# Building the one-hot tables of a mixture-of-experts placement column by column on VectorE and GpSimd

## The reference, cut to what matters

```
logits = xf @ Wg
idx = jnp.argmax(logits, axis=-1)
final = jnp.zeros_like(xf)
for e in range(N_EXPERTS):
    y = geglu(xf, W1[e], W2[e], W3[e])
    final = final + jnp.where((idx == e)[:, None], y, 0.0)
return (shared + final).reshape(B, T, C)
```

## Time and profile before

| | |
|---|---|
| median of 3 runs | 1822.69 us (1822.34 to 1825.03) |
| the profiled execution's own time | 1825.35 us |
| span of that execution in the profile | 1823.4 us |
| TensorE busy | 1508.2 us, 83% of the span |
| VectorE busy | 1206.4 us, 66% |
| GpSimd busy | 1014.5 us, 56% |
| ScalarE busy | 953.0 us, 52% |
| placing in the first shared stage | 72 to 103 us of the span |
| placing in the second shared stage | 1020 to 1052 us |
| placing in the routing of the top-2 mixture | 1240.4 to 1262.8 us |

### The profile page before, as it was taken

How to read it: one execution, slowest core, us unless ns; L and a number is a source line. 1 busy time by engine, 2 the same in 40 slices (tenths; PEclk the granted TensorE clock), 3 DMA queues, 4 the chain that set the end, 5 groups by cost and what they waited for, 6 DMA issues and landing times. The chain is left out here.

```text
span 1823.4 us, 36275 instructions
## 1 busy us (share of the span) xinstructions
PE 1508.2 (83%) x9925; PEld 1265.2 (69%) x9988; DVE 1206.4 (66%) x2802; ACT 953.0 (52%) x1970; POOL 1014.5 (56%) x1326
## 2 busy tenths in 40 slices
PE   6889956699999999999978899943999378809993
PEld 4559953478888888888765579942999256708993
DVE  5535556689999999999745545557566368724566
ACT  2213334678787777878733223342666267616662
POOL 2135742188888888888862146644543474553442
PEclk9999976799999999999988999955999689959997
DMA  7001130101010110101106011160222121112224
GB/s 248 1 24 32 47 107 29 37 26 38 26 38 26 30 33 26 37 26 38 37 1 202 1 29 41 41 201 7 69 66 57 39 53 32 36 36 62 64 62 157
DMA packets 112428, 98.53 MB, mean 54 GB/s; under 512 B 25312, under 2 KB 88960, under 8 KB 112288
## 3 DMA queue, kind: packets, MB, share of 16 engines
q1 hardware_dynamic: 97424, 68.84, 12.7%
q0 software_dynamic: 13632, 27.98, 5.5%
q10 hardware_dynamic: 1232, 0.04, 0.0%
HBM read 50.24 MB, written 44.47 MB: 52 GB/s over the span
## 5 line engine op out<-in xcount | busy, mean ns | idle before, releaser
L886 PE MATMUL ps<-gT,w_slot 128*128 128x128 f32 x1760 | 242.4, 282 | 4.5 <-ACT gT L920 3.2
L898 PE MATMUL ps<-w,inner_slot 128*128 x1760 | 235.5, 277 | 5.5 <-DVE inner_slot L976 3.2
L886 PEld LDWEIGHTS ps<-gT,w_slot 128*128 128x128 f32 x1760 | 219.4, 196 | 13.7 <-issue 6.0
L898 PEld LDWEIGHTS ps<-w,inner_slot 128*128 128x128 f32 x1760 | 213.9, 192 | 10.5 <-issue 9.8
L1966 DVE SCALAR_TENSOR_TENSOR xbc<-ps,cw,xbc 128x1021 f32<-128x1021 f32 x132 | 168.3, 1275 | 16.8 <-ACT xbc L1845 14.7
L966 DVE TENSOR_TENSOR hb<-ps,b 128x512 f32<-128x512 f32 x142 | 98.2, 691 | 105.3 <-PE ps L886 96.6
L831 POOL DMA_INDIRECT rows_in<-xn_rows,slot_token x117 | 113.6, 971 | 81.0 <-PE ps L874 56.5
L1720 PE MATMUL ps<-xnT,win 128*128 128x512 f32 x256 | 134.2, 650 | 27.1 <-DVE xbc L1966 21.5
L2158 POOL TENSOR_TENSOR xd<-t,xd 128x256 f32<-128x256 f32 x128 | 94.3, 736 | 86.6 <-DVE t L2001 86.6
L1771 PEld LDWEIGHTS ps<-XB,LM 128*128 128x128 f32 x1024 | 136.1, 194 | 6.8
L838 POOL DMA_INDIRECT y_rows<-y,slot_row x78 | 91.1, 1168 | 81.0 <-DVE y L983 79.8
(11 more groups left out here) (336 smaller groups left out, 4011.0 us busy)
## 6 DMA issues: line engine op xcount, KB each, us to landing
sorted_rows<-blank SPq DMA_DIRECT2D x33, 516.0 KB, 4.8
w<-in_L_ffn_W SPq DMA_DIRECT2D x5, 2048.0 KB, 10.7
xn_rows<-xn SPq DMA_DIRECT2D x24, 256.0 KB, 4.3
xn<-y_rows SPq DMA_DIRECT2D x24, 256.0 KB, 5.2
rows_in<-sorted_rows SPq DMA_DIRECT2D x71, 64.5 KB, 1.8
y_rows<-y SPq DMA_DIRECT2D x71, 64.0 KB, 1.5
rows_in<-xn_rows,slot_token POOLq DMA_INDIRECT x149, 2.6
x<-in_L_attn_x SPq DMA_DIRECT2D x8, 256.0 KB, 6.4
```

Of the source, the lines that this page charges most:

```text
L886: ins = nc.tensor.matmul(h1[:, u, b * P:(b + 1) * P], w[:, b * P:(b + 1) * P], k.gT[:, r, :], start=True, stop=True)
L898: ins = nc.tensor.matmul(py[:, q % 2, :], k.inner_slot[:, q % RING, b * P:(b + 1) * P], w_dn[:, ds(e * (FB * D) + b * D, D)], start=(b == ...
```

## The change

`match` and ScalarE's part are gone. VectorE makes each column on its own: one operation on the list of slot numbers compares with `hi` and multiplies by the partition number straight into `oh_slot`, a second compares lanes. GpSimd does the same with the tile number as a constant. So GpSimd no longer waits for VectorE batch by batch: it waits once until `hi` is there, which VectorE signals behind `route_positions`, and then only for `placed`. A batch is now 8 VectorE operations in place of 2, 4 on GpSimd in place of 1, and none on ScalarE.

```diff
@@ route: vector
             route_positions(k, do, top)
+            dve.sem_inc(k.matched.sem, 1)
             for n in range(NB):
-                match_vector(k, dve, n, slots)
+                match_vector(k, dve, n, slots, top)
@@ route: scalar
             nc.scalar.activation(k.small[:, 0:NT], k.small[:, 0:NT], ACT.Exp).then_inc(expd.sem, 1)
-            for n in range(NB):
-                match_lanes(k, act, n, slots, top)
@@
-def match_vector(k, dve, n, slots):
+def match_vector(k, dve, n, slots, top):
     V, r = k.nc.vector, n % 2
-    cols = slice(n * GRP, (n + 1) * GRP)
-    dve.wait_ge(k.lanes_put.sem, k.lanes_put.at(n - 1))
-    dve.wait_ge(k.tiles_put.sem, k.tiles_put.at(n - 1))
-    V.tensor_tensor(k.match[:, r, :, 0:slots], bcast(k.iota_bf[:, 0:slots], 1, GRP), bcast(k.hi[:, cols], 2, slots),
-                    ALU.is_equal).then_inc(k.matched.sem, 1)
     dve.wait_ge(k.placed.sem, k.placed.at(n - 1))
-    V.tensor_tensor(k.oh_lane[:, r, :, :], bcast(k.iota_bf[:, 0:P], 1, GRP), bcast(k.lo[:, cols], 2, P),
-                    ALU.is_equal).then_inc(k.onehot.sem, 1)
-def match_lanes(k, act, n, slots, top):
-    r = n % 2
-    act.wait_ge(k.matched.sem, k.matched.at(n + 1))
-    act.wait_ge(k.placed.sem, k.placed.at(n - 1))
-    k.nc.scalar.activation(k.oh_slot[:, r, :, 0:slots], k.match[:, r, :, 0:slots], ACT.Copy,
-                           scale=k.lane[:, top - 1:top]).then_inc(k.lanes_put.sem, 1)
+    for j in range(GRP):
+        c = n * GRP + j
+        V.tensor_scalar(k.oh_slot[:, r, j, 0:slots], k.iota_bf[:, 0:slots], k.hi[:, c:c + 1], k.lane[:, top - 1:top],
+                        ALU.is_equal, ALU.mult)
+        ins = V.tensor_scalar(k.oh_lane[:, r, j, :], k.iota_bf[:, 0:P], k.lo[:, c:c + 1], None, ALU.is_equal)
+    ins.then_inc(k.onehot.sem, 1)
 
 def match_tiles(k, pool, n, slots):
     r = n % 2
-    pool.wait_ge(k.matched.sem, k.matched.at(n + 1))
+    if n == 0:
+        pool.wait_ge(k.matched.sem, k.matched.at(1))
     pool.wait_ge(k.placed.sem, k.placed.at(n - 1))
-    k.nc.gpsimd.tensor_tensor(k.oh_slot[:, r, :, slots:2 * slots], k.match[:, r, :, 0:slots],
-                              bcast(k.tile_of[:, n * GRP:(n + 1) * GRP], 2, slots), ALU.mult
-                              ).then_inc(k.tiles_put.sem, 1)
+    for j in range(GRP):
+        c = n * GRP + j
+        ins = k.nc.gpsimd.tensor_scalar(k.oh_slot[:, r, j, slots:2 * slots], k.iota_bf[:, 0:slots], k.hi[:, c:c + 1],
+                                        float(c + 1), ALU.is_equal, ALU.mult)
+    ins.then_inc(k.tiles_put.sem, 1)
@@ place_tensor
     pe.wait_ge(k.onehot.sem, k.onehot.at(n + 1))
-    pe.wait_ge(k.lanes_put.sem, k.lanes_put.at(n + 1))
     pe.wait_ge(k.tiles_put.sem, k.tiles_put.at(n + 1))
@@ shared: vector
                 if u == 15:
                     route_positions(k, do, 1)
+                    dve.sem_inc(k.matched.sem, 1)
                 if 16 <= u < 24:
-                    match_vector(k, dve, u - 16, slots)
+                    match_vector(k, dve, u - 16, slots, 1)
@@ shared: scalar
-                if 17 <= u < 25:
-                    match_lanes(k, act, u - 17, slots, 1)
```

More of the change, by code:

```diff
@@ L459, in place_counters @@
     k.onehot, k.placed, k.place_own = (k.counter(f"place_{n}") for n in ("onehot_ready", "done", "step"))
-    k.matched, k.lanes_put, k.tiles_put = (k.counter(f"place_{n}") for n in ("matched", "lanes_put", "tiles_put"))
+    k.matched, k.tiles_put = (k.counter(f"place_{n}") for n in ("matched", "tiles_put"))
 def close_places(k, batches, top):
-    for s in (k.onehot, k.placed, k.matched, k.lanes_put, k.tiles_put):
+    for s in (k.onehot, k.placed, k.tiles_put):
         s.close(batches)
+    k.matched.close(1)
@@ L2263, in setup @@
     k.oh_lane, k.oh_slot = S("oh_lane", [P, 2, GRP, P], BF16), S("oh_slot", [P, 2, GRP, 2 * SLOTS2], BF16)
-    k.iota_bf, k.match = S("iota_bf", [P, P], BF16), S("match", [P, 2, GRP, SLOTS2], BF16)
+    k.iota_bf = S("iota_bf", [P, P], BF16)
     k.wg0, k.wg1, k.bg = S("wg0", [P, NE]), S("wg1", [P, NE]), S("bg", [P, NE])
```

## The result

The changed kernel took 1834.36 us (median of 10 runs, 1829.17 to 1837.96). The kernel before, run beside it, took 1824.92. The ratio is **1.0042, 95% interval [1.0028, 1.0057]**: slower by 0.4%, which is some 7.7 us. The forecast was 4.3 us faster.

What follows compares the result with a forecast made beforehand. ScalarE's weighing was taken to stall TensorE in the shared stages, VectorE to bound the routing. Shared stages -8.2, routing +3.9, together -4.3: 1822.69 to 1818.4 us; range 1810 to 1833, the forecast's own 1812 to 1824.

Steps and rivals of the forecast that it cites:

- The step that failed: Routing: GpSimd's four operations per batch take at most 1.36 us, under M, if the extra [128, 1] operand is cheap.
- M: VectorE's time from first to last operation of a batch: forecast 1.70 us in the routing, 1.55 in the shared stage.
- rival D: Routing: GpSimd becomes the bound; 0.5 an operation gives 1823.2 us, 0.7 gives 1836; chance 20%.
- the 1.01 for a power of four elements: Profile row of a GpSimd power, 1.01 us, beside which VectorE's four operations took 1.08, no more than their own sum.
- The lower bound for free [128, 1] operands: VectorE's batch if its [128, 1] operands cost nothing: given as 4 x 0.24 = 0.96 us.
- rival C: New VectorE operations cost 1.0 ns per element, batch 2.02 + 0.25 and 1.89 + 0.15: 1831.5 us; chance 10%.
- The contention of 0.25 and 0.15: What GpSimd's four operations add to VectorE's batch: 0.25 us in the routing, 0.15 in the shared stage.
- Rival B: GpSimd holds up every new VectorE operation for its whole duration, batch 2.80 and 2.57: 1844 us; chance 9%.
- Forecast -4.1: Each shared stage: TensorE waits for VectorE's table instead of ScalarE's weighing, gain 10.3 - 4M = 4.1 us.
- the 1.0 that the forecast called lost behind the last placing: Shared stage: `inner(25)` stands behind the table of experts, so 1.0 us of the last placing's 1.29 is lost.
- rival E: Shared stages give nothing because something unseen ends them, and the routing's +3.9 remains: 1826.6 us; chance 6%.
- The forecast's 0.4: End of the routing: L369 no longer meets GpSimd's last table, saving 0.4 us.

Runs made afterwards that it cites:

- kernel 1: Changed kernel plus a stretch ahead of all work timing series of eight single operations on GpSimd, VectorE, then both; whole took 1866.56 us, left out of comparisons.
- kernel 6: Changed kernel plus a stretch of GpSimd alone, series of eight varying output offset, column and constants; series take 4.12 to 4.75 us, no whole time given.
- kernel 4: Changed kernel, but in the routing VectorE makes the tile part of two of four columns instead of GpSimd; stretch 41.7 to 34.5, execution 1823.9 us (one run).
- kernel 5: Changed kernel, but GpSimd's routing operation multiplies instead of comparing, so its tables are wrong; routing stretch 41.7 to 28.6 us, one run 1816.0.
- kernel 8: New tables in shared stages, old in routing, where ScalarE also weighs two of four tile columns; 1810.77 us, ratio 0.9921 against the kernel before the change.
- kernel 2: Changed kernel with the old tables put back in the routing, new ones kept in both shared stages; 1813.57 us, ratio 0.9939 against the kernel before the change.

## Why the prediction was wrong, point by point

**The step that failed** is the one on GpSimd in the routing: "GpSimd: alone, one input of 4 elements takes 0.23; 71 elements at 0.0016 add 0.11: four are at most 1.36, under M, if the extra [128, 1] operand is cheap." It took the price per element from a product of two inputs and gave it to a comparison, and called the sum a maximum. The operand that it named as its condition is indeed cheap. The forecast was 0.34 an operation; the comparing form alone takes 0.52 (kernel 1), and the routing's 64 took 0.604 each. Of the 0.26 that was missing, about half is the price of an element (71 times 0.0034 in place of 0.0016), 0.05 the fixed part (0.28 for 0.23), and 0.09 comes on top in place, part of which the series with changing constants show too (kernel 6). Four take 2.25 to 2.53, over M, so GpSimd sets the pace. The prediction had named this as a sign of being wrong: a GpSimd operation over 0.4.

This is rival D, which had 20%. Its working from that point was right in kind: at 38.65 / 64 = 0.604 an operation, its formula gives 16 x (2.42 - 1.43) - 0.4 = +15.4 for the routing, and +14.3 was measured. The missing 1.1 is more than explained by `route_experts`, which D left behind the tables and which is hidden beside GpSimd's last ones (-2.1). That this one term is the cause is shown from both sides: kernel 4 took half of it away and kernel 5 made it cheap, and the routing fell to 34.5 and 28.6.

I had a row that ought to have widened the bound, the 1.01 for a power of four elements, and used it for VectorE's contention and for the rival's chance, not for this term.

**VectorE's batch, M.** The uncontended part was right to 0.04: 1.44 and 1.41 forecast, 1.48 measured with 71 slots and 1.44 with 39 (95.98 to 97.51, less 0.09 for the overlap, where GpSimd rests). Single operations were forecast at 0.29 and 0.25 and take 0.30 and 0.25 in the probe. (The lower bound for free [128, 1] operands is 4 x 0.21 = 0.84 by the prediction's own terms, not 0.96; nothing else uses it.) The Trainium skill (VectorE: DVE Perf Modes, "The perf-mode tier table") gives a bf16 `tensor_scalar` four elements a cycle. These durations fit it, with the prediction's fixed parts, to 0.02; rival C and its 1.0 ns per element are out. The contention of 0.25 and 0.15 was too much: with GpSimd at work all the time the batch was 1.48 in kernel 5, as alone. In the change itself it was mostly 1.67 in the first half of the routing (1244.25 to 1246.01, less 0.09) and 1.53 to 1.56 in most of the second. So the comparison on GpSimd disturbs VectorE there and the product of kernel 5 does not. It lies in GpSimd's shadow and costs nothing.

**Rival B, the lock.** The Trainium skill (SBUF — State Buffer, "Who interferes with whom") says that a VectorE operation in a two-port mode and GpSimd exclude each other for the whole instruction. For the new forms no run shows that: 12 pairs beside GpSimd's eight take 0.39 each against 0.37 alone. Whole-instruction exclusion would have added 8 x 0.54 to them. In kernel 5 GpSimd's operation goes from 0.32 to 0.37 and VectorE's batch stays as it is alone. The same section says that a VectorE instruction with two SBUF inputs contends with GpSimd's reads; with that the old form agrees, in the earlier trace rows and in kernel 8.

**Shared stage.** Forecast -4.1, measured -3.7, and the parts can be checked against start times. From the first placing to the eighth: 29.18 before (73.40 to 102.58), 24.19 now (76.85 to 101.04), -5.0. From the end of the positions to the first: 3.49 before, 3.75 now, +0.3, where the forecast had no change. From the eighth to `slot_row`: 4.34 before, 5.34 now, +1.0, which is the 1.0 that the forecast called lost behind the last placing. There `inner(25)` stands behind `route_experts`, and TensorE waits for it:

```profile
104.59 0.24 DVE L380 CAST slot_expert<-erow 128x156 int32<-128x156 f32 x1
104.86 0.69 DVE L600 TENSOR_TENSOR inner<-gl,ps 128x512 f32<-128x512 f32 x1
...
105.61 1.12 PE L705 MATMUL ps<-xnT,w 128*128 128x512 f32 x2 [0.75 <-DVE inner L600]
```

So rival E is out, and the gain reaches the end of the kernel (kernel 2). GpSimd's four were held to be hidden "while they take under 4 us together": they took 2.0, and were.

**Routing, the rest.** L369 still runs beside a GpSimd operation (1272.36, GpSimd's starts at 1272.38), but this one does not hold it: 0.25 now, 0.65 before. The forecast's 0.4 is there, in the shadow of GpSimd.

**The sum.** With GpSimd out of the way the forecast would have been on the safe side: in kernel 5, which differs in GpSimd's operation alone, the stretches add up to -7.5 + 1.1 = -6.4 against before, where -4.3 was forecast. Its one run took 1816.0. Its tables are not the right ones, so what comes behind them is no fair comparison.

## What to carry to other kernels

When work moves from one operation on four columns to four operations, price it on each engine from an operation of the same kind; a price per element from a product says nothing about a comparison. Where no row shows the operation, the upper bound belongs into the sum's range and has to be held against the engine that is forecast to bind: here 1.48 / 4 = 0.37 an operation was the point at which GpSimd overtook VectorE, and the estimate stood at 0.34. The same change can win where an engine has slack (here 2.0 us of GpSimd in a shared stage, where placings are 2.1 to 5.5 apart) and lose in a short loop of 1.4 us, so it is worth making it per stage.

## What was not expected of the hardware

- GpSimd, `tensor_scalar` on 128x71 bf16: compare and multiply 0.52, comparison alone 0.44, product and product 0.32, `tensor_tensor` product 0.27. A single product by a constant takes 0.46.
- The same operation on GpSimd is followed after 0.52 or after 0.62, depending on its constants: eight with one constant take 4.12 to 4.18, eight with the constants 1 to 8 take 4.75, of which the first two cost nothing more. Another [128, 1] column costs nothing, an odd output element costs nothing.
- A second [128, 1] operand on GpSimd is no way round it: 0.60 from start to start with VectorE at work.
- VectorE's and GpSimd's `tensor_scalar` forms on bf16 run side by side at 0.39 against 0.37 a pair, while the `tensor_tensor` forms of the kernel before end one after another.
